# Expert inputs scattered as bf16 halves and loaded by transposing transfers

## The reference

```
x = x + attention(layernorm(x), ctx, ctx, length)      # 2048 rows of 256, 16 heads of 64, 1601 keys, rotary positions, masked keys
x = x + moe(layernorm(x))
moe(y): scores = y @ gate_w.T; softmax over 8 experts; the two largest, their weights scaled to sum 1
        each expert: (silu(y @ w1.T) * (y @ w3.T)) @ w2.T      # 256 -> 512 -> 256
        result = weighted sum of the two chosen experts' outputs
```

## Time and profile before

| what | value |
|---|---|
| timed runs | 1206.67, 1209.41, 1213.72 us; median 1209.41 |
| profiled execution, span from first to last instruction | 1211.3 us |
| mean granted TensorE clock | 0.965 |
| mixing stage, last load of attention output begins | about 906 us |
| first load of the expert loop issued | 1004.4 us |
| first accumulating store | 1028.3 us |
| last accumulating store | 1202.3 us |

### The profile page before, as it was taken

One profiled execution on the slowest core, in us unless ns is written; L12 is line 12 of the kernel. 1 busy time (PEld: TensorE's weight loads), 2 busy tenths in 40 slices (PEclk: granted clock), 3 DMA queues, 4 the chain that ended last, 5 costly groups with the idle time before them and its releaser, 6 DMA issues. The chain is left out here.

```text
span 1211.3 us, 32849 instructions
## 1 busy us (share of the span) xinstructions
PE 1070.4 (88%) x12843; PEld 709.2 (59%) x13030; DVE 979.4 (81%) x1769; ACT 731.4 (60%) x1298; POOL 644.6 (53%) x457
## 2 busy tenths in 40 slices
PE   1468999999999999999999999999969958999995
PEld 1334566566656656656665665666648944566663
DVE  5878999999999999999999999999944674455552
ACT  2635666666666666666666666766644643455552
POOL 1045764674585477467448647733449554333333
PEclk9679999999999999999999999999988979999998
DMA  8034242332423324143242433317526522333330
GB/s 280 0 97 115 79 107 63 98 91 69 107 79 97 96 81 104 51 122 84 77 99 76 110 79 90 79 38 224 207 99 231 174 84 84 57 52 57 54 60 12
DMA packets 104445, 117.01 MB, mean 97 GB/s; under 512 B 47389, under 2 KB 86494, under 8 KB 103006
## 3 DMA queue, kind: packets, MB, share of 16 engines
q1 hardware_dynamic: 91214, 99.74, 29.5%
q0 software_dynamic: 7152, 8.43, 4.2%
q10 hardware_dynamic: 5920, 6.65, 2.0%
HBM read 39.46 MB, written 36.87 MB: 63 GB/s over the span
## 5 line engine op out<-in xcount | busy, mean ns | idle before, releaser
L829 ACT ACTIVATE prob<-sc,key_bias 128x512 f32<-128x512 f32 x640 | 405.3, 684 | 149.2 <-PE sc L683 145.1
L962 DVE TENSOR_REDUCE part_max<-mx 128x1 f32<-128x427 f32 x768 | 417.3, 590 | 35.8 <-PE mx L700 35.8
L1106 POOL TENSOR_TENSOR prob_lo<-prob 128x1024 bf16<-128x1024 f32 x128 | 242.5, 1894 | 229.4 <-ACT prob L829 229.3
L974 DVE TENSOR_TENSOR prob_lo<-prob 128x1024 bf16<-128x1024 f32 x192 | 278.2, 1449 | 9.8 <-ACT prob L829 6.2
L727 PE MATMUL pv<-VV,prob 128*128 128x65 bf16 x2560 | 267.9, 193 | 3.7 <-POOL prob_lo L1106 3.5
L729 PE MATMUL pv<-VV,prob_lo 128*128 128x65 bf16 x2560 | 269.3, 195 | 0.0
L728 PE MATMUL pv<-VV,prob 128*128 128x64 bf16 x2560 | 268.0, 193 | 0.0
L727 PEld LDWEIGHTS pv<-VV,prob 128*128 128x128 bf16 x2560 | 239.8, 99 | 38.8 <-POOL prob_lo L1106 7.3
L728 PEld LDWEIGHTS pv<-VV,prob 128*128 128x128 bf16 x2560 | 237.2, 97 | 26.4
L683 PE MATMUL sc<-Q,K 65*128 65x512 bf16 x640 | 243.6, 381 | 10.3 <-issue 4.0
L700 PE MATMUL mx<-K,Q 128*128 128x427 bf16 x768 | 236.6, 349 | 9.7 <-DVE part_max L962 5.1
(11 more groups left out here) (208 smaller groups left out, 1470.8 us busy)
## 6 DMA issues: line engine op xcount, KB each, us to landing
expert_inputs<-zeros SPq DMA_DIRECT2D x129, 129.0 KB, 2.8
we<-in_w_exp SPq DMA_DIRECT2D x8, 1536.0 KB, 7.9
Q<-we SPq DMA_DIRECT2D x45, 256.0 KB, 3.8
attention_out<-o_out SPq DMA_DIRECT2D x64, 128.0 KB, 2.0
o_in<-attention_out SPq DMA_DIRECT2D x16, 512.0 KB, 3.7
q32s<-q SPq DMA_DIRECT2D x122, 64.0 KB, 2.0
K<-we SPq DMA_DIRECT2D x48, 160.0 KB, 3.9
VV<-next_v SPq DMA_DIRECT2D x16, 322.5 KB, 4.0
```

The source lines that it names most:

```text
L829: act.activation(prob[:, s % PRING, j, :], sc[n % 2][:], ACT.Exp, bias=key_bias[:, t:t + 1], scale=HD ** -0.5).then_inc(exp_done, 1)
L962: dve.tensor_reduce(part_max[:, b_ % 2, qt, h:h + 1], mx[:, pl.part_banks(qt, h)[0]:pl.part_banks(qt, h)[-1] + 1, 0:pl.width], mybir.AxisL ...
L974: dve.tensor_tensor(prob_lo[:, s % PRING, 0:g, :], prob[:, s % PRING, 0:g, :], hi_half(prob[:, s % PRING, 0:g, :])[:, :, 1::2], ALU.subtra ...
L1106: pool.tensor_tensor(prob_lo[:, s % PRING, 0:g, :], prob[:, s % PRING, 0:g, :], hi_half(prob[:, s % PRING, 0:g, :])[:, :, 1::2], ALU.subtr ...
```

## The change

The normalised row is no longer kept in `yrows` as 256 floats. ScalarE writes it to `y32`, two buffers deep, and then writes its bf16 rounding to the first half of the row's 1,024 bytes; VectorE writes the rest (value minus rounding, in bf16) to the second half, as the first instruction of the step after. A row of `expert_inputs` then holds 256 high halves, 256 low halves, the number and the weight, in the same 1,032 bytes. `scatter_low` waits for the low halves (`y_lo_made`) instead of `nm_made`. TensorE's transposes for the gate read `y32`.

In the expert loop SyncE issues two transfers for a tile: a transposing one that brings the 128 rows of 512 bf16 values as four blocks of 128x128 into `xT`, now six buffers deep, and a small one that brings number and weight into `row_ends`, 8 bytes from each of 128 rows. `high_x`, `split_x` and both `turn_x` go, with PSUM tile `pxt`. The load of tile i waits for `up3_ready` of tile i-6 in place of `xt_ready`. TensorE waits for both transfers before the first matmul of a tile.

```diff
-        x_in = sb("x_in", [P, TURN, RW])
-        x_hi = sb("x_hi", [P, 2, D], BF16)
-        x_lo = sb("x_lo", [P, 2, D], BF16)
+        y32 = sb("y32", [P, 2, D])
+        y_halves = yrows[:].bitcast(BF16)[:, :, 0:2 * D]
+        slot_halves = x_slots.bitcast(BF16)[:, 0:2 * D]
+        row_ends = sb("row_ends", [P, TURN, RW - D])
-        xT = sb("xT", [P, 2, 2, DT, P], BF16)
+        xT = sb("xT", [P, TURN, 2 * DT, P], BF16)
...
@@ SyncE: fetch and load
-                    sp.dma_start(x_in[:, i % TURN, :], x_slots[bass.ds(row, P), :]).then_inc(x_tile[i % TURN], 16)
+                    sp.dma_start_transpose(xT[:, i % TURN, :, :], slot_halves[bass.ds(row, P), :]).then_inc(x_tile[i % TURN], 16)
+                    sp.dma_start(row_ends[:, i % TURN, :], x_slots[bass.ds(row, P), D:RW]).then_inc(x_tile[i % TURN], 16)
-                    need(sp, xt_ready, q, TURN, i - TURN + 1)
+                    need(sp, up3_ready, q, TURN, i - TURN + 1)
@@ ScalarE, mixing stage, t = step - 3
-                        act.activation(yrows[:, t, 0:D], x1[:, t, :], ACT.Identity, scale=rstd[:, t % 2:t % 2 + 1],
+                        if t >= 2:
+                            act.wait_ge(yt_ready, t - 1)
+                            act.wait_ge(y_lo_made, t - 1)
+                        act.activation(y32[:, t % 2, :], x1[:, t, :], ACT.Identity, scale=rstd[:, t % 2:t % 2 + 1],
                                        bias=shift[:, t % 2:t % 2 + 1]).then_inc(nm_made, 1)
+                        act.wait_ge(nm_made, t + 1)
+                        act.activation(y_halves[:, t, 0:D], y32[:, t % 2, :], ACT.Copy).then_inc(y_hi_made, 1)
@@ ScalarE, expert loop: high_x and its calls go; results reads row_ends
-                                   scale=x_in[:, i % TURN, D + 1:D + 2]).then_inc(y_made, 1)
+                                   scale=row_ends[:, i % TURN, 1:2]).then_inc(y_made, 1)
@@ GpSimd
-                    pool.wait_ge(nm_made, QT * (c + 1))
+                    pool.wait_ge(y_lo_made, QT * (c + 1))
...
-                    pool.wait_ge(x_tile[i % TURN], 16 * (i // TURN + 1))
+                    pool.wait_ge(x_tile[i % TURN], 32 * (i // TURN + 1))
...
-                    ids = x_in[:, i % TURN, :].bitcast(I32)[:, D:D + 1]
+                    ids = row_ends[:, i % TURN, :].bitcast(I32)[:, 0:1]
@@ VectorE, first in each step of the mixing stage
+                    t = step - 4
+                    if 0 <= t < ST:
+                        dve.wait_ge(y_hi_made, t + 1)
+                        dve.tensor_tensor(y_halves[:, t, D:2 * D], y32[:, t % 2, :], y_halves[:, t, 0:D], ALU.subtract).then_inc(y_lo_made, 1)
@@ VectorE, expert loop: split_x and turn_x and their calls go
@@ TensorE
-                            ins = pe.transpose(yt[:, d, :], yrows[:, t, d * P:(d + 1) * P], ident)
+                            ins = pe.transpose(yt[:, d, :], y32[:, t % 2, d * P:(d + 1) * P], ident)
...
-                    need(pe, xt_made, q, TURN, i + 1)
                     if which == 0:
+                        pe.wait_ge(x_tile[i % TURN], 32 * (i // TURN + 1))
                         need(pe, silu_made, q, TURN, i)
...
-                        ins = pe.matmul((p1, p3)[which][:], xT[:, i % 2, h, d, :],
+                        ins = pe.matmul((p1, p3)[which][:], xT[:, i % TURN, h * DT + d, :],
@@ TensorE, expert loop: turn_x (four transposes of x_hi and x_lo) and its calls go
```

More of the change, by code:

```diff
@@ L1415, in project_and_mix @@
         p1, p3 = banks[0], banks[1]
-        pxt = banks[2].bitcast(BF16)[:, 0:2 * D].rearrange("p (h d c) -> p h d c", h=2, d=DT)
         pht = [bank.bitcast(BF16).rearrange("p (h f c) -> p h f c", h=2, f=FT) for bank in (banks[3], wp[1][:])]
@@ L1423, in project_and_mix @@
         hid_hi_made = sem("hid_hi_made")
-        x_hi_made, x_lo_made, xt_ready, xt_made = sem("x_hi_made"), sem("x_lo_made"), sem("xt_ready"), sem("xt_made")
+        y_hi_made, y_lo_made = sem("y_hi_made"), sem("y_lo_made")
         up1_ready, up3_ready = sem("up1_ready"), sem("up3_ready")
@@ L1534, in silu @@
                     act.activation(act_s[:, i % 2, :], p1[:], ACT.Silu).then_inc(silu_made, 1)
[L1536 to L1540, removed]
                 def high_hidden(i):
@@ L1562, in turn @@
                         results(j - 1, q)
-                        if j + 2 < tiles_.stop:
-                            high_x(j + 2)
                 act.sem_inc(y_made, 2)
                 act.sem_inc(ht_hi_made, 1)
-                high_x(0)
-                high_x(1)
                 silu(0)
                 high_hidden(0)
-                high_x(2)
                 body(turn, act)
@@ L1783, in _ @@
                 weigh_high(3)
[L1785 to L1791, removed]
                 def hidden(i, q=0):
@@ L1810, in turn @@
                         hidden(j, q)
-                        if not last or j + 1 < tiles_.stop:
-                            turn_x(j + 1, q)
                         low(j, q)
-                        if j + 2 < tiles_.stop:
-                            split_x(j + 2)
                 dve.sem_inc(hid_made, 1)
                 dve.sem_inc(ht_lo_made, 1)
-                split_x(0)
-                turn_x(0)
-                split_x(1)
                 hidden(0)
-                turn_x(1)
                 low(0)
-                split_x(2)
                 body(turn, dve)
@@ L1913, in warm_up @@
                         pe.matmul(p1[:], ident_b[:], wo_hi[:, 0:2, :].rearrange("p j n -> p (j n)"), start=True, stop=True)
-                def turn_x(i, q=0):
-                    need(pe, x_lo_made, q, TURN, i + 1)
-                    need(pe, xt_made, q, TURN, i)
-                    for d in range(DT):
-                        pe.transpose(pxt[:, 0, d, :], x_hi[:, i % 2, d * P:(d + 1) * P], ident_b[:])
-                    for d in range(DT):
-                        ins = pe.transpose(pxt[:, 1, d, :], x_lo[:, i % 2, d * P:(d + 1) * P], ident_b[:])
-                    ins.then_inc(xt_ready, 1)
                 def up(expert, which, i, q=0):
-                    need(pe, xt_made, q, TURN, i + 1)
                     if which == 0:
+                        pe.wait_ge(x_tile[i % TURN], 32 * (i // TURN + 1))
                         need(pe, silu_made, q, TURN, i)
```

## The result

The changed kernel takes 1230.26 us (median of 4 runs, 1227.3 to 1232.19) beside 1211.14 us for the kernel before on the same chip: a ratio of 1.0156, 95% interval 1.0127 to 1.0186, so 19 us slower. The forecast was 1217.7 us in a range of 1208 to 1246, with 0.69 on slower. The sign and the range held, and both places where time was to be lost were named; but the time lies above the 1211 to 1226 us of the forecast's own case, and the loss is 2.3 times the 8.3 us forecast, because a third place was counted at nothing and the loop's term was too small.

A forecast was written before the change was run, and what follows sets the result against it. The prediction took the expert loop's chain of accumulating stores as the bound: 1211.3 + 0 + 4.8 + 3.5 = 1219.6 us of span, less 1.9 us, forecast 1217.7 us, in a range of 1208 to 1246.

The forecast's parts named there:

- the forecast's own case: Whole kernel: the main forecast of 1217.7 us, with its own range of 1211 to 1226 us and chance 0.58.
- Stores bind, not TensorE: Expert loop: GpSimd's accumulating stores, 4.68 us apart, set its end, beside TensorE's 4.73 us a tile.
- All 39 show it: Expert loop: claim that every store is issued only after the previous landed; GpSimd waited 32 times for a store's DMA.
- Part 1: Expert loop: removing halves, transposes and copy cuts TensorE's tile from 4.73 to about 4.46 us, but counts 0.
- Part 2, the end of the stage: End of mixing stage: VectorE's subtraction queued first delays the ScalarE-VectorE handover; costs 4.8 us, bounds 0 and 6.
- the step table: Mixing steps 16 to 18: worked-out times by which choosing for tiles 8 to 11 starts 5.3 us later.
- The rival in which the handing over hides: End of mixing stage: ScalarE's copy overlaps VectorE's work, so the 4.8 us vanish, giving 1212.9 us; chance 0.12.
- in steps that TensorE fills both engines have a third of time free, so I count 0 there: Mixing stage: the added ScalarE copy (0.41 us) and VectorE subtraction (0.43 us) per row tile cost nothing.
- Part 3: Expert loop's load: the new transfers stay longer and fall on the store's packets; +0.1 us a tile, 3.5 us.
- the row of 2.0 us to landing: Attention stage's 128 KB write to o_dram in 256-byte pieces, taken as lower bound for the transposing transfer's landing.
- The slow-transfer rival: Expert loop: the transposing transfer stays some 1 us longer, costing 31 us instead of 3.5, so 1245 us; chance 0.20.
- Store 0 near 1033: Start of expert loop's stores: sign of a right forecast, the first store near 1033 us; 1028 would show it wrong.

The follow-up runs named there:

- e3: Changed kernel plus one unread 512-column TensorE matmul per tile; 1229.98 us, 1.0139 of the kernel before.
- e6: Changed kernel with all stores' rows sent out of bounds, so nothing is added to the output; 1214.41 us, 1.0027 of the kernel before.
- e5: Kernel before with all stores' rows sent out of bounds, so nothing is added to the output; 1207.02 us, 0.9964 of the kernel before.
- e1: Changed kernel's mixing stage and scatters, but tiles loaded plainly and transposed on TensorE; 1222.62 us, 1.0100 of the kernel before.
- e10: Changed kernel whose transposing transfer brings only the high halves, 64 KB instead of 128; 1222.95 us, 1.0110 of the kernel before.
- e8: Kernel before with SyncE's two register loads moved ahead of the wait for the store's landing; 1210.42 us, 0.9994 of the kernel before.
- e13: Kernel before with register loads ahead of the wait and scatters paced every four tiles instead of two; 1207.58 us, 0.9963 of the kernel before.
- e9: Changed kernel with GpSimd's 16 weight subtractions cut into 64 shorter ones; 1254.80 us, 1.0358 of the kernel before.
- e2: Changed kernel's expert loop, but no halves made in the mixing stage and a constant scattered instead; 1221.77 us, 1.0089 of the kernel before.
- e4: Changed kernel with VectorE's subtraction moved from the start of each mixing step to its end; 1220.11 us, 1.0065 of the kernel before.
- e7: e4 with SyncE's two register loads moved ahead of the wait for the store's landing; 1214.86 us, 1.0027 of the kernel before.

## Why the prediction was right, step by step

- **Stores bind, not TensorE.** Right, and shown for the changed kernel: e3 adds TensorE time for nothing, e6 takes the stores' work away and gains 15.8 us. In the kernel before the two were nearly level: e5 gains 4.6 us, then TensorE's results set the pace. "All 39 show it" was read too strongly from 32 waits; it is the lag that carries it.
- **Part 1 counts 0.** Right. The size was off: 0.14 us a tile between results (e5, e6), not 0.27. The start was off too: 4.73 us came from two tiles, while the earlier trace rows put the results of tiles 0 to 34 at (1181.51 - 1017.74) / 34 = 4.82 us apart. So TensorE's tile after is 4.62 us (e6), not 4.46, only 0.06 under the stores' 4.68. From 4.82 us the saving of 0.27 would have led to 4.55; the missing 0.07 us is as much as TensorE idles in e6 (busy for 98.6%), but what it waits for there was not separated.
- **Part 2, the end of the stage: +4.8 us.** Right in mechanism, and in size with some luck. B is 37.3 to 37.4 us in the five kernels that put the subtraction first and leave GpSimd's weight split as it was (after, e1, e3, e6, e10) and 32.6 to 32.8 in e5, e8 and e13, which make no halves: 4.7 us. (e9, held up by its one long subtraction, has 34.8.) From the first scatter to the choosing for tiles 8 to 11 it is 25.3 us in those five and 19.9 in those three, 5.3 us more, as worked out. In the profiled pair that choosing began at 990.20 where it was 983.42, but these 6.8 us hold A too:

```profile
989.79 0.42 DVE L1738 TENSOR_TENSOR yrows<-y,yrows 128x256 bf16<-128x256 f32 x1 [1.85 <-ACT yrows L1523]
990.20 0.17 DVE L1661 TENSOR_REDUCE top<-logits 128x4 f32<-128x32 f32 x1
```

  The profiled execution of before, from which the step table was worked out, had a B of 36.2 us, so this pair alone gives 1.2 us for this step and would have made it look wrong; that the table's difference fits the other kernels better than its own is the luck. Why B was longer there is open (its VectorE idled for 2.1 us before L1689 at 974.77, and no releaser is named). The profile after also began the stage 2.3 us sooner, at 917.27 instead of 919.56; together these leave only 3.3 us between the two at store 0, though A alone grew by 6.1. A difference of two single profiles was not enough here. The rival in which the handing over hides falls.
- **Part 2, "in steps that TensorE fills both engines have a third of time free, so I count 0 there".** This is the step that failed. A rose by 6.1 to 8.1 us in the same five kernels (it is 41.6 in before, e5, e8 and e13, which make no halves and write no constant into the rows). A share of free time says nothing of what an instruction costs that needs what another engine holds: 0.43 us by the earlier trace rows, which came from a stretch where GpSimd does no arithmetic, against 2.60 us here. The two large two-operand VectorE instructions of this stage in the kernel before (L1751, L1759) each read one operand from PSUM, and the statistics read one operand only, so this stage had no such collision to show; but it did show GpSimd busy for 26 of the 41 us, and I priced by ScalarE's and VectorE's columns alone.
- **Part 3, +0.1 us a tile.** The mechanism was right (packets of the load over those of the store, handed on by each store), the term too small: 0.30 us a tile (4.97 against 4.68), 34 x 0.30 = 10 us in the profiled pair; 7 us by e2 without its own cost. I had the transfer near the row of 2.0 us to landing; it measured 3.5, near the upper end of 3.9, of which 1.23 us are its issue. Nor does a later landing count in full, as the range had it: 1.4 us more of it would have been 1.4 us a tile, and e10 lands after 3.4 us with an interval of 4.71. What counts is how many packets fall behind the start of the store's. Here the load's begin 1.7 us after the store's issue, where they began after 1.0; that the longer issue, which I counted at nothing, is what moved them fits this but was not tested apart. The slow-transfer rival (0.9 us a tile) has the same mechanism and was to decide from about 0.3 us a tile: the truth lies at that border, and the range held it because of this rival.
- **The sum.** 4.8 + 3.5 = 8.3 us was forecast. e1 puts the mixing stage at 11.4 and e2 the loop at some 7; together they come near the 19 us measured. "Store 0 near 1033" came true (1031.6), but by a B that was long before and an early start after; in the other four of the five kernels it is 1034 to 1037.

## What to carry to other kernels

Before an instruction is put into an engine's spare time, look at what the other engines do in the same stretch, not only at that engine's busy share, and put it behind whatever a neighbour waits for: e4's change of order alone gave back 10 us of 19. Where a loop ends in transfers that wait for each other, compare the lag between a result and its store at the first and the last tile; if it does not shrink to nothing, work saved in the loop is worth nothing, and what another transfer puts on top of the stores' packets is paid for once a tile. How long that transfer takes to land doesn't tell how much this is; its packets' place in time does. A stage's length is better read over several kernels' traces than from one pair.

## What the runs showed of the hardware

- A VectorE subtraction of 128x256 with both operands in SBUF took 0.42 us alone, 2.60 us beside GpSimd instructions of 2.75 us, and, once, 31.36 us beside 64 of them of about 0.78 us (e9): cutting GpSimd's work into shorter instructions made the wait longer. A comparison of 32 columns, 0.19 us otherwise, took 3.58 us in the same way, over a boundary between two GpSimd instructions of 2.75 us (e2).
- A transposing transfer of 128x512 bf16 held SyncE's queue for 1.23 us, against 0.34 to 0.41 us for a plain one, and landed after 3.5 us, or 2.7 us where it was issued clear of the store (e7).
- Accumulating stores with no row in bounds still came 4.44 us apart in e6, and 3.9 us over the first eight intervals of e5 (1023.5 to 1054.6): most of the interval is issuing and waiting for the landing, not the 128 KB.
